# Graph network on Trainium2: the radial functions of pass 2 with every third group instead of every second, and its sums cleared behind the first part

## The reference, cut to what matters

```python
def _L1_gnn_ref(x, edge_index, edge_attr, W1n, b1n, W2n, b2n, W1e, b1e, W2e, b2e, gin_eps, rms_w):
    ...
    edge_msg = jax.nn.relu(edge_attr @ W1e + b1e) @ W2e + b2e
    messages = (x[src] + edge_msg) * edge_weight[:, None]
    agg = jax.ops.segment_sum(messages, dst, num_segments=n)
    ...
def _L2_gnn_ref(node_feats, edge_vec, edge_length, senders, receivers, ...):
    ...
    rhat = edge_vec / (jnp.linalg.norm(edge_vec, axis=-1, keepdims=True) + 1e-12)
    emb = _radial_embedding(edge_length)
```

## Time and profile before

| | |
|---|---|
| median of the runs | 4595.72 us (3 runs, 4593.0 to 4596.33) |
| profiled execution | 4596.9 us |
| its span | 4592.8 us |
| busy: PE / DVE / ACT / POOL | 81% / 72% / 62% / 71% of the span |
| chain that ended last | POOL 30%, issue 22%, PE 13%, DVE 12%, ACT 11% |
| second edge pass | from 1174 us of the span to about 2235 us |

### The profile page before, as it was taken

The page is one execution under the profiler, slowest core; times in us unless marked ns, Lnnn a source line. Parts: engine busy times, 40 slices in busy tenths (PEclk is TensorE's granted clock), DMA queues, the critical chain, the costliest instruction groups (busy, mean ns, idle before and its releaser), DMA issues.

```text
span 4592.8 us, 103410 instructions
## 1 busy us (share of the span) xinstructions
PE 3703.2 (81%) x25659; PEld 3151.5 (69%) x25659; DVE 3297.4 (72%) x7523; ACT 2863.7 (62%) x7389; POOL 3272.3 (71%) x3433
## 2 busy tenths in 40 slices
PE   6888888887376666666879888888887999999996
PEld 5555555555376666666757777777777888888886
DVE  5766666666554444444668777777777999999998
ACT  3777767775532222222467666666656888888887
POOL 5777777775677777777657777777747777777772
PEclk8988888897587778777979999999989999999998
DMA  8888888884443333333122222222228878888882
GB/s 253 243 240 233 239 234 235 238 232 137 115 99 76 82 80 78 82 76 82 46 63 57 56 56 56 56 56 56 56 75 244 236 234 234 235 234 235 235 234 82
DMA packets 645300, 676.45 MB, mean 147 GB/s; under 512 B 126720, under 2 KB 511294, under 8 KB 645054
## 3 DMA queue, kind: packets, MB, share of 16 engines
q0 software_dynamic: 132928, 327.04, 27.2%
q1 hardware_dynamic: 511390, 347.67, 25.4%
q10 hardware_dynamic: 864, 0.39, 0.0%
HBM read 583.98 MB, written 89.08 MB: 147 GB/s over the span
## 4 chain that ended last, share of the span: by engine, by line
POOL 30%; issue 22%; PE 13%; DVE 12%; ACT 11%; DMA 7%; ACTq 2%; SPq 1%; DVEq 1%; POOLq 1%
POOL e_rows L877 21%; POOL xt L877 9%; PE banks L940 7%; ACT e_away L917 4%; DVE acc L964 4%; DMA xt<-up_t,e_index 3%; PE banks L1058 3%; DVE banks L1508 3%; ACT e_logit L1504 1%; ACT banks L1570 1%; DMA e_q_rows<-q_t 1%; PE banks L449 1%; ACTq L970 1%; ACT e_rows L1569 1%; ACT e_rise L1540 1%
## 5 line engine op out<-in xcount | busy, mean ns | idle before, releaser
L964 DVE TENSOR_TENSOR acc<-acc,banks 128x256 f32 x3328 | 1379.3, 414 | 887.8 <-PE banks L940 753.5
L877 POOL DMA_INDIRECT xt<-up_t,e_index x799 | 757.1, 948 | 243.5 <-issue 213.1
L877 POOL DMA_INDIRECT e_rows<-x_t,e_index x771 | 730.2, 947 | 246.6 <-issue 233.2
L877 POOL DMA_INDIRECT e_rows<-fsv_t,e_index x771 | 730.5, 947 | 235.1 <-issue 217.4
L877 POOL DMA_INDIRECT e_rows<-kv_t,e_index x771 | 730.3, 947 | 235.1 <-issue 223.7
L1200 ACT ACTIVATE e_rows<-banks,e_rows 128x128 f32<-128x128 f32 x832 | 237.0, 370 | 723.6 <-DMA e_rows<-x_t,e_index 467.4
L940 PE MATMUL banks<-e_sel,e_msg 128*128 128x128 f32 (+1 forms) x3328 | 653.1, 311 | 0.0
L1191 PE MATMUL banks<-e_w,xt 65*128 65x128 f32 x1664 | 271.4, 316 | 350.6 <-DMA xt<-in_attr_rows 345.6
L940 PEld LDWEIGHTS banks<-e_sel,e_msg 128*128 128x128 f32 (+1 forms) x3328 | 355.6, 147 | 262.0 <-issue 171.8
L917 ACT ACTIVATE e_away<-node_iota,local 128x128 f32<-128x128 f32 x1664 | 525.9, 388 | 0.0
L1191 PEld LDWEIGHTS banks<-e_w,xt 65*128 65x128 f32 x1664 | 247.5, 228 | 359.3 <-issue 314.0
(11 more groups left out here) (194 smaller groups left out, 7016.0 us busy)
## 6 DMA issues: line engine op xcount, KB each, us to landing
e_q_rows<-q_t SPq DMA_DIRECT2D x832, 64.0 KB
sel_d<-e_sel_t SPq DMA_DIRECT2D x208, 256.0 KB
e_sel_t<-sel_d SPq DMA_DIRECT2D x208, 256.0 KB
e_far<-fdst_t SPq DMA_DIRECT2D x832, 64.0 KB
e_near<-near_d SPq DMA_DIRECT2D x208, 128.0 KB
xt<-in_attr_rows SPq DMA_DIRECT2D x208, 128.0 KB, 3.4
e_resets<-reset_d SPq DMA_DIRECT2D x208, 128.0 KB
xt<-up_t,e_index POOLq DMA_INDIRECT x799
```

The source lines that it names most:

```text
L877: G.indirect_dma_start(out=self.rows[0:n, u, i, 0:self.width], out_offset=None, in_=self.table, in_offset=bass.IndirectOffsetOnAxis(ap=ind ...
L964: V.tensor_tensor(to, to, bank[n_bank][:, col:col + W].rearrange("p (k d) -> p k d", k=2), ALU.add).then_inc(self.s_added[i], 1)
```

## The change

```diff
-            if not cleared:
-                V.memset(acc[:], 0.0).then_inc(self.zeroed, 1)
+            if cleared is False:
+                self.clear()
             if fixed:
                 for e in (PE, V, A):
                     e.wait_ge(self.s_load, self.loads)
+
+        def clear(self):
+            V.memset(acc[:], 0.0).then_inc(self.zeroed, 1)
...
-                elif not self.cleared:
+                elif self.cleared is not True:
                     V.wait_ge(self.zeroed, 1)
...
-            ATTRS = 5
+            ATTRS, RADIAL = 5, 3
...
-            ps = EdgePass(ctx, x1_t, D + 1, own=D, sels=2, sel=sel, fixed=
+            ps = EdgePass(ctx, x1_t, D + 1, own=D, sels=2, sel=sel, cleared=None, fixed=
...
-                if not isinstance(g.n, int) or g.n % 2 or g.n // 2 >= CHUNK_TILES:
+                if not isinstance(g.n, int) or g.n % RADIAL or g.n // RADIAL >= CHUNK_TILES:
                     return
-                q = g.n // 2
+                q = g.n // RADIAL
...
                 me = v.did(V.tensor_tensor(emb, emb, inside.unsqueeze(1).to_broadcast([P, NB, P]), ALU.mult))
+                if not q:
+                    ps.clear()
                 wait(A, mt, *([(d_rhat, d_rhat.at)] if q else []))
```

## The result

The changed kernel took 4602.8 us, the kernel before 4593.8 us in the same comparison (medians of 20 runs each): a ratio of 1.0019, 95% interval 1.0012 to 1.0025. That is 9.0 us more, where 9.7 were forecast; 9.2 us, or 0.2%, was the line that the prediction drew between slower and no change, and the result lies just under it. The profiled execution of the changed kernel has a span of 4597.2 us.

What follows compares the result with a forecast made beforehand. GpSimd's gathers bound the kernel, stopped only by index waits; a new 14 us wait at group 25 replaces 11.6 us, moving it from 1315.6 to 1325.3: 4595.7 + 9.7 = 4605.4 us median, range 4594 to 4611.

Steps and rivals of the forecast that it cites:

- slower: Whole kernel: time up by over 0.2% (9.2 us), chance 0.42.
- Gather 25 carries the change: GpSimd, second edge pass: shift of group 25's first gather moves the kernel's end by as much, +9.7 us.
- within 0.2%: Whole kernel: time changed by no more than 0.2% (9.2 us), chance 0.44.
- The closed loop: Part, stores, attribute load, hidden and sums, additions, next part: 21.45 us per three-group part; chance 0.66.
- the 5.2: TensorE, start of `hidden` to end of `sums`: 5.2 us, between 5.48 (idle 4 us) and 4.88 (idle 9 us).
- the 0.7 us for the index load: SyncE step 10: index load stands ahead of group 10's attributes and costs the loop 0.7 us once.
- The clear: VectorE memset of 10.72 us moved behind the first part: first part 11.2 us earlier, second only 5.1.
- Group 15: GpSimd, second pass: its index load lands earlier, so group 15 starts at 1259.4, 3.9 us earlier.
- Group 25: GpSimd: index load issued at 1321.1, lands 4.25 us later; start 1325.3 after a new 14 us wait.
- (1): Rival: VectorE's own work paces the parts, period 15.6, both index waits go, -11.6 us, 4584; chance 0.14.
- (2): Rival: loop closes but shorter, attribute load 4.15 us, period 20.3, +4 us, 4600; 0.20 shared with (3) and page's rule.
- (3): Rival: third group doesn't slow parts, period 19.5, effects cancel, 4596; 0.20 shared with (2) and page's rule.

Runs made afterwards that it cites:

- g1_attr_ahead: Changed kernel with SyncE's attribute loads issued two groups ahead: 4579.7 us, ratio 0.9972 to the kernel before in the same job.
- h4_before_attr_ahead: Kernel before (parts every second group, clear ahead of the pass) with attribute loads two groups ahead: ratio 0.9995 to the kernel before.

## Why the prediction was right, step by step

- **Gather 25 carries the change.** Right: it moved by 10.0 us, the pass's last gather by 8.8, the median by 9.0. But the median's 9.0 is less than the 9.2 that the prediction put as 0.2%, so by its own words this falls in "within 0.2%" (0.44), by a hair, and not in "slower" (0.42).
- **The closed loop.** Right in mechanism and size. Period 21.45 forecast; the stores of the second to the seventh part (36.3 to 144.1 us into the pass) are 21.6 apart in the mean, 21.0 to 22.3. Its terms, in the five turns from the second part to the seventh: floats' issue to `hidden` 4.82 to 5.68 (5.14 in the mean), 4.95 forecast; `hidden` to the end of the sums 4.73 to 5.49, 5.2 forecast (5.21 in the mean). The two rows behind the 5.2 seemed to say that this term is shorter after a longer idle time of TensorE. It isn't so here: the shortest, 4.73, came after the shortest idle time, 5.94 us, and after the longest, 8.29, it was 5.21. The mean hit; that reading of two cases did not hold. Nor did the 0.7 us for the index load ahead of group 10's attributes show: that turn has the shortest first term, 4.82. `g1_attr_ahead` shows the cause, `h4_before_attr_ahead` that it is absent with two groups to a part.
- **The clear.** The term that was mis-sized: 10.72 was taken from the row, and it is 13.34 with the idle time ahead of it. The 0.48 us ahead of the smaller memset in the rows was a hint, small enough to pass for a gap. Of the 2.6 us, 1.0 was made up again: the first part was done 0.5 us earlier than worked out, and the selects behind the clear took less. The second part ended 36.2 us into the pass, not 34.6.
- **Group 15.** 3.9 us earlier was forecast, 1.3 came: 1.6 of the difference is that of the second part, 1.1 comes from two periods of 21.7 and 22.3.
- **Group 25.** The index load was issued 3.12 us after the last part, 3.0 forecast, but the gather started 2.9 after that issue instead of 4.25, below the bounds of 3.8 to 4.7. That gave back the 1.4 us by which the parts were late. Two errors of opposite sign: that 10.0 came so close to 9.7 is in part luck.
- **What was not forecast.** One wait of 14 us was expected, ahead of group 25; two came, and 4.1 of theirs fell to group 24, which waited for the sums of group 14. With seven microseconds to a group, TensorE had fallen behind GpSimd by all of the ten slots. It changed nothing here, since the indices for group 25 came later still.
- **Rivals.** (1) didn't happen here, and `g1_attr_ahead` shows its period (15.6) and about its gain: 11.6 us less than before were worked out, 12.9 measured (4579.7 against 4592.7 in that job). In its trace the last gather comes 13.4 us earlier: 11.6 are the waits of before, 1.2 the quicker gathers behind group 25, and 0.6 the gathers of before that took longer ahead of it. (2) had the attribute load at 4.15 us; it was 4.8 and more in each turn, and no period was under 21.0, so (2) and the 19.5 of (3) didn't come about. The estimate of 2.9 us worked out in the prediction from the Trainium skill (DMA: Bandwidth & Descriptors, "Anatomy of one DMA") lies further off still; here the loads stood behind two embedding stores, the direction store and the floats.

## What to carry to other kernels

A side job that is spread over more steps of a pipeline can become slower than its own work, as here: 21.6 us a part, where VectorE's work alone takes 15.6. The parts were tied together by a transfer of the main work. So ask, for each part of such a job, which main result the next part is queued behind, and whether that result needs a transfer that stands behind this part in a DMA queue. If so, issue the transfer further ahead first (here two groups, which turned +0.24% into -0.28% in job g, and gained nothing over the kernel before in jobs e and f). And a load that is needed at a fixed step, such as the indices for group 25, makes the end of the whole side job count: work out when its last part ends, not only how fast it goes.

## What was not expected of the hardware

A memset's row on VectorE is shorter than the memset. 12800, 6400 and 2560 elements have rows of 10.72, 5.39 and 2.19 us and idle time of 2.62, 1.28 and 0.48 us ahead: 13.34, 6.67 and 2.67, each 1.04 us per 1000 elements. And the same program took about 4593 us in two jobs and 5753 to 5843 us on three other chips, where single instructions of TensorE stood 1.4 us apart with nothing to wait for. The attributes two groups ahead were 0.28% faster than before in job g, 0.03% in job f (an interval that holds 1), and 0.15% slower in job e.
